# The next batch's token transposes go to the bank of the probabilities' transposes

## The chip, the cores and the metric

The kernel runs on one core of one Trainium2 chip. The metric is device time in microseconds of one execution; before and after are compared by medians of several runs.

## The reference

The reference is one transformer block over 16 batches of 256 tokens with 128 features, in float32. The attention half is what the change touches:

```
x = _layernorm(x)
q, k, v = x Wq, x Wk, x Wv            # 16 heads of 64
scores  = q k^T / sqrt(64), causal
attn    = softmax(scores)
heads   = attn v
y       = x + heads Wo, then a layernorm with gamma and beta
x       = x + _layernorm(y)
```

Then follows a router over 8 experts (softmax of `xt @ router_w`, the top 2), an expert layer `gelu(xt @ w1[e]) @ w2[e]` weighted with the gates, a last layer norm, and a residual sum.

## The kernel before

Attention runs over the 16 batches (`b`), each in four steps (`u` = 0 to 3), each step for two pairs of heads (`p`, `p + 1`; `k` counts steps over all batches). After the attention the expert part works on tiles of 256 rows. The order of the work is written out by hand for each engine, and the engines meet through semaphores.

Everything in one step is a pipeline over several engines. TensorE (the function `step` in the tensor block) does in this order: Q and K of the pair two ahead (`qk_proj`, L385 to L387, three products of split float32 values), the transposes of the normalised probabilities of an earlier pair (`p_transpose`, L442 to L447), the output projection (`w_o`, L434), the next `qk_proj`, the next `p_transpose` and `w_o`, a part of V (`v_proj`, L385 to L387 with 512 columns), the product of probabilities and V (`pv_two`, L423), and then scores and masks (L406, L409, L414) of the two next pairs. In step 1 of a batch it also does the transposes of the router's rows (L453), the router's logits (L460) and, between `pv_two` and the scores, the two 128x128 transposes of the next batch's tokens (`x_transpose`, L378).

ScalarE in the same step: the copy of Q and K out of PSUM (`qk_copy`, L1263), the exponentials of two pairs (L1268, L1274; each has an accumulator read behind it), the copies of the transposed probabilities (`pT0_copy`, L1279), the copy of V (`v_copy`, L1283), the copy of the attention's output (`o_copy`, L1288), and in step 1 the copy of the transposed tokens (`xt_copy`, L1258) and the router's exponential (L1297). VectorE: maxima of the scores (L777, L778), the division of the probabilities (L788, L792), the second half of the transposes' copies (L798), the norms (L755 for the tokens), and the split of the transposed tokens into a high and a low part (`x_split`, L770 and L772) in step 2.

PSUM has eight banks of 512 float32 per partition. Four hold scores (`SC`), and there is one each for `PT0` (transposes of the probabilities, in front of `pT0_copy`), `PT1O` (further transposes, and the attention's output), `M` (Q, K and V projections, and so far the token transposes) and `A` (output projection, router).

Semaphores that the text names: `v_done` counts copies of V; `xt_mm` and `xt_st` count token transposes and their copies; `xn_done` normalised tokens; `qk_sb` copies of Q and K; `exp_done` pairs whose exponentials are done; `pt0_sb` copies out of PT0; `nrm` normalised pairs; `xt_split` splits.

Of the kernel before, what the change touches and what calls it, by code (L numbers as in the profile page):

```python
# [14 lines left out]
P = 128  # L15
# [5 lines left out]
def sandwich_kernel(nc, x, wq, wk, wv, wo, gamma, beta, router_w, w1, w2, out):  # L21
    B, S, D = x.shape
    H, _, E = wq.shape
    NE, _, F = w1.shape
    T = S // P
    NP = H // 2
# [32 lines left out]
    with ExitStack() as ctx:  # L59
        def sb(name, shape, dt=F32):  # L60
            return ctx.enter_context(nc.sbuf_tensor(name, shape, dt))

        def bank(name):
            return ctx.enter_context(nc.psum_tensor(name, [P, 512], F32))
# [3 lines left out]
        def sem(name):  # L68
            if name not in sems:
                sems[name] = ctx.enter_context(nc.semaphore(name))  # L70
            return sems[name]
# [16 lines left out]
        ident = sb("ident", [P, P])  # L88
# [10 lines left out]
        xn = [sb(f"xn{n}", [P, T, D]) for n in range(2)]  # L99
        xt_st = sb("xt_st", [P, S])  # L100
# [87 lines left out]
        PT0, PT1O, M, A = (bank(n) for n in ("PT0", "PT1O", "M", "A"))  # L188
# [19 lines left out]
        v_mm, v_done = sem("v_mm"), sem("v_done")  # L208
# [14 lines left out]
        def before_out(attending):  # L223

            first = T * D if attending else T * D + 2 * T * NE
            return A[:, first:first + (T + 1) * NE]
# [14 lines left out]
        def there(b, back=0):  # L241

            return not isinstance(b, int) or 0 <= b - back < B
# [9 lines left out]
        def is_last(b):  # L253

            return isinstance(b, int) and b == B - 1
# [116 lines left out]
        def _(pe):  # L372
            mm = nc.tensor.matmul

            def x_transpose(b):
                pe.wait_ge(sem("xn_done"), b + 1)
                for t in range(T):
                    last = nc.tensor.transpose(M[:, t * P:(t + 1) * P], xn[b % 2][:, t, :], ident[:])  # L378
                last.then_inc(sem("xt_mm"), 1)

            pe.wait_ge(sem("ident_ok"), 1)
            x_transpose(0)

            def product3(dst, a_hi, a_lo, b_hi, b_lo, start=True):
                mm(dst, a_hi, b_hi, start=start, stop=False, skip_group_check=True)  # L385
# [3 lines left out]
            def qk_proj(c, dst=M):  # L389

                cs = slice(c * P, (c + 1) * P)
                for i in range(2):
                    last = product3(dst[:, i * S:(i + 1) * S], wqk_hi[:, i, cs], wqk_lo[:, i, cs],
                                    xt_hi[:], xt_lo[:], start=(i == 0))
                last.then_inc(qk_mm, 1)

            def v_proj(t, half_of_heads):
                cols = slice(half_of_heads * 512, half_of_heads * 512 + 512)
                ts = slice(t * P, (t + 1) * P)
                product3(M[:, :], xt_hi[:, ts], xt_lo[:, ts], wv_hi[:, cols], wv_lo[:, cols]).then_inc(v_mm, 1)  # L400
# [30 lines left out]
            def w_o(c):  # L431
                par = c % 2
                for t in range(T):
                    last = mm(A[:, t * D:(t + 1) * D], hT[:, par, t * P:(t + 1) * P], wo_sb[:, c, :],  # L434
                              start=(c == 0 and t == 0), stop=(c == NP - 1), skip_group_check=True)
                if c == NP - 1:
                    last.then_inc(sem("wo_mm"), 1)

            def p_transpose(p):
                slot, par = p % 4, p % 2  # L440
                for k in range(2):
                    last = nc.tensor.transpose(PT1O[:, par * S + k * P:par * S + (k + 1) * P], prob[:, slot, k, 2, :],  # L442
                                               ident[:])
                last.then_inc(t1_mm, 1)
                for k in range(2):
                    nc.tensor.transpose(PT0[:, k * S:k * S + P], prob[:, slot, k, 0, :], ident[:])  # L446
                    last = nc.tensor.transpose(PT0[:, k * S + P:(k + 1) * S], prob[:, slot, k, 1, :], ident[:])  # L447
                last.then_inc(t0_mm, 1)

            def rows_transpose(dst, r):  # L450
                pe.wait_ge(sem("xf_done"), r + 1)
                for t in range(T):
                    last = nc.tensor.transpose(dst[:, t * P:(t + 1) * P], xf[:, t, :], ident[:])  # L453
                last.then_inc(sem("xfT_mm"), 1)
# [25 lines left out]
            def step(b, u):  # L480


                k = STEPS * b + u
                p = 2 * k
                c = 2 * u
                more = u < STEPS - 1 or there(b, -1)

                if u == 1 and there(b, 2):
                    pe.wait_ge(pt0_sb, p - 2)
                    rows_transpose(PT0, b - 2)  # L490

                if more:
                    if k >= 1:
                        pe.wait_ge(v_done, 4 * b + 1 + u)
                    if u == 2 and there(b, -1):
                        pe.wait_ge(sem("xt_st"), b + 2)
                    if u == STEPS - 1:
                        pe.wait_ge(sem("xt_split"), b + 2)
                    if k == 1:
                        pe.wait_ge(sem("wqk_lo"), 4)  # L500
                    qk_proj((c + 2) % NP)

                if k >= 1:
                    pe.wait_ge(nrm, p - 1)
                    if k >= 2:
                        pe.wait_ge(o_sb, k - 1)
                        pe.wait_ge(pt0_sb, p - 2)
                    if u == 1 and there(b, 2):
                        pe.wait_ge(sem("xfT_sb"), b - 1)
                    p_transpose(p - 2)  # L510

                if k == 0:
                    pe.wait_ge(qk_sb, 3)
                    v_proj(0, 0)


                if k >= 2:
                    pe.wait_ge(o_sb, k - 1)
                    if u == 2 and there(b, 1):
                        pe.wait_ge(sem("att_done"), b)  # L520
                        if there(b, 2):
                            pe.wait_ge(sem("lg_done"), b - 1)
                    if u == 1 and there(b, 3):
                        pe.wait_ge(sem("before_sb"), b - 2)
                    w_o((c - 4) % NP)

                if more:
                    pe.wait_ge(qk_sb, p + 3)
                    if k == 0:
                        pe.wait_ge(v_done, 1)  # L530
                    qk_proj((c + 3) % NP)

                if k >= 1:
                    pe.wait_ge(nrm, p)
                    pe.wait_ge(pt0_sb, p - 1)
                    pe.wait_ge(pt1_sb, p - 1)
                    p_transpose(p - 1)

                if k >= 2:
                    w_o((c - 3) % NP)  # L540
                if u == 0 and there(b, 3):
                    rows_before(b - 3, before_out(True), False)
                if u == 1 and there(b, 2):
                    logits(b - 2, logits_out(True), False)
                if is_last(b) and u == STEPS - 1:
                    first_rows()

                turn = v_turn(b, u)
                if turn:
                    if more:  # L550
                        pe.wait_ge(qk_sb, p + 4)
                    v_proj(turn[0], turn[1])

                if k >= 1:
                    pe.wait_ge(pt0_sb, p)
                    pe.wait_ge(pt1_sb, p)
                    pe.wait_ge(v_done, 4 * b if u == 0 else 4 * b + 2 if u < 3 else 4 * b + 4)
                    pv_two((c - 2) % NP)


                if u == 1 and there(b, -1):
                    pe.wait_ge(v_done, 4 * b + 3)
                    x_transpose(b + 1)

                if more:
                    pe.wait_ge(qk_sb, p + 4)
                    pe.wait_ge(exp_done, p + 1)
                    scores(0)
                    pe.wait_ge(exp_done, p + 2)
                    scores(1)  # L570
                    masks(0)
                    masks(1)
# [155 lines left out]
            for g in range(NG):  # L728
# [3 lines left out]
                for r in range(K):  # L732
                    last = mm(sum_bank[g % 4][:], ident[:], zz[:, g % 4, r].rearrange("p t d -> p (t d)"),
                              start=(r == 0), stop=(r == K - 1))
# [517 lines left out]
        @block.scalar  # L1252
        def _(act):
            a = nc.scalar
            def xt_copy(b):
                act.wait_ge(sem("xt_mm"), b + 1)

                a.activation(xt_st[:].rearrange("d (p t) -> d t p", t=T), M[:, 0:S].rearrange("d (t p) -> d t p", t=T),  # L1258
                             ACT.Copy).then_inc(sem("xt_st"), 1)

            def qk_copy(p, src=M):
# [49 lines left out]
                        .then_inc(sem("wqk_h"), 1)  # L1311

            qk_high(0)
            xt_copy(0)
            act.wait_ge(sem("wv_ld"), 16)
            a.activation(wv_hi[:], wv_in[:], ACT.Copy).then_inc(sem("wv_h"), 1)
            qk_copy(0)
# [323 lines left out]
```

## Time and profile before

| | |
|---|---|
| median of 3 runs | 734.25 us (733.94 to 735.72) |
| profiled execution | 735.79 us |
| its span | 734.0 us |
| TensorE busy | 687.1 us, 94% of the span |
| VectorE busy | 553.2 us, 75% |
| ScalarE busy | 521.7 us, 71% |
| mean granted TensorE clock | 0.984 |

The span is the time from the profile's first to its last instruction; the device time holds a little more. Busy time is time in which the engine works on an instruction; the ends of matmuls are modelled, so starts are the safer numbers.

### The profile page before, as it was taken

How to read it: one execution, taken by the hardware profiler on the slowest of the kernel's cores; microseconds unless marked ns; L12 is line 12 of the kernel's file. 1: busy time of each engine (PE TensorE's matmuls, PEld its weight loads, DVE VectorE, ACT ScalarE, POOL GpSimd, SP SyncE). 2: the span in 40 equal slices, each digit the busy share in tenths (PEclk: the TensorE clock that was granted, in tenths of full speed). 3: DMA queues.
4: the chain of work that ended last, by engine and by line, in shares of the span. 5: the costliest groups of instructions: out<-in, count | busy, mean ns of one | idle time of the engine just before them, and what ended most of it. 6: DMA issues, size and time to landing. Idle time of an engine off the chain costs nothing.

```text
span 734.0 us, 17696 instructions
## 1 busy us (share of the span) xinstructions
PE 687.1 (94%) x5954; PEld 593.1 (81%) x5955; DVE 553.2 (75%) x1914; ACT 521.7 (71%) x1687; POOL 273.2 (37%) x388
## 2 busy tenths in 40 slices
PE   4899999999999999999999999999989999999954
PEld 3688878888888888887888888888868999999921
DVE  5667889888797989888887989898886775444216
ACT  4787777888787877888877878788765664555515
POOL 3022634332323232332323231322322877655535
PEclk9999999999999999999999999999999999999978
DMA  7530000000000000000100000000020234322155
GB/s 182 173 87 8 9 8 12 21 21 18 24 8 23 9 24 8 25 15 16 31 8 23 9 23 8 24 15 10 21 56 24 73 104 132 91 74 84 41 184 174
DMA packets 43701, 34.88 MB, mean 48 GB/s; under 512 B 10624, under 2 KB 40320, under 8 KB 43616
## 3 DMA queue, kind: packets, MB, share of 16 engines
q1 hardware_dynamic: 37984, 23.81, 12.1%
q0 software_dynamic: 4544, 9.45, 3.6%
q8 instruction: 47, 0.77, 0.4%
q10 hardware_dynamic: 1088, 0.54, 0.3%
q14 instruction: 38, 0.31, 0.1%
HBM read 20.22 MB, written 13.56 MB: 46 GB/s over the span
## 4 chain that ended last, share of the span: by engine, by line
PE 65%; ACT 14%; DVE 12%; DMA 3%; issue 3%; POOL 2%; DVEq 1%; SPq 0%; POOLq 0%; ACTq 0%
PE M L684 8%; PE SC L406 8%; PE PT1O L423 8%; PE A L434 5%; PE M L385 4%; ACT prob L1274 4%; PE M L387 4%; PE M L386 4%; PE SC L414 4%; PE SC L409 3%; ACT prob L1268 3%; ACT qk L1263 3%; PE PT1O L442 2%; PE SC L385 2%; PE SC L386 2%
## 5 line engine op out<-in xcount | busy, mean ns | idle before, releaser
L1263 ACT ACTIVATE qk<-M 128x512 f32<-128x512 f32 x127 | 75.9, 598 | 90.0 <-PE M L387 90.0
L1274 ACT ACTIVATE prob<-SC,nmax 128x256 f32<-128x256 f32 x256 | 125.7, 491 | 0.0
L423 PE MATMUL PT1O<-pT,v_sb 128*64 128x256 f32 (+1 forms) x1024 | 98.6, 335 | 0.7 <-ACT pT L1279 0.7
L423 PEld LDWEIGHTS PT1O<-pT,v_sb 128*64 128x64 f32 x1024 | 64.1, 138 | 42.8 <-ACT pT L1279 17.2
L1268 ACT ACTIVATE prob<-SC,nmax 128x128 f32<-128x128 f32 x256 | 95.4, 382 | 3.4 <-DVE nmax L778 3.3
L1544 POOL DMA_INDIRECT expert_rows<-v_sb,got x78 | 77.1, 988 | 46.5 <-ACT v_sb L1418 27.7
L788 DVE TENSOR_TENSOR prob<-prob,rden 128x512 f32<-128x512 f32 x128 | 88.8, 694 | 2.4 <-DVE rden L782 0.2
L1533 POOL DMA_INDIRECT sent_rows<-rec,slot x64 | 66.6, 1040 | 57.7 <-DVE slot L1038 39.3
L778 DVE TENSOR_REDUCE nmax<-SC 128x2 f32<-128x512 f32 x128 | 86.9, 679 | 0.0
L385 PE MATMUL M<-xt_hi,wqk_hi 128*128 128x256 f32 x254 | 82.5, 325 | 3.0 <-DVE xt_lo L772 2.2
L406 PE MATMUL SC<-qk 64*128 64x256 f32 x512 | 84.4, 406 | 0.6 <-ACT prob L1274 0.6
L777 DVE TENSOR_REDUCE nmax<-SC 128x2 f32<-128x256 f32 x128 | 53.1, 415 | 38.6 <-PE SC L414 38.3
L1279 ACT ACTIVATE pT<-PT 128x512 f32<-128x512 f32 x128 | 76.6, 598 | 3.3 <-PE PT L447 3.3
L434 PE MATMUL A<-wo_sb,hT 128*128 128x128 f32 x512 | 77.8, 275 | 0.0
L684 PE MATMUL M<-w_sb,hidT 128*128 x624 | 76.2, 275 | 0.9 <-ACT v_sb L1418 0.9
L684 PEld LDWEIGHTS M<-w_sb,hidT 128*128 128x128 f32 x624 | 72.7, 192 | 1.1 <-issue 1.1
L387 PE MATMUL M<-xt_hi,wqk_lo 128*128 128x256 f32 x254 | 72.1, 284 | 0.0
L386 PE MATMUL M<-xt_lo,wqk_hi 128*128 128x256 f32 x254 | 71.6, 282 | 0.0
L434 PEld LDWEIGHTS A<-wo_sb,hT 128*128 128x128 f32 x512 | 67.1, 192 | 0.0
L447 PE MATMUL PT<-ident,prob 128*128 128x128 f32 x256 | 62.8, 273 | 0.0
L446 PE MATMUL PT<-ident,prob 128*128 128x128 f32 x256 | 62.8, 273 | 0.0
L1418 ACT ACTIVATE v_sb<-M,got 128x128 f32<-128x128 f32 x78 | 24.4, 364 | 52.3 <-PE M L684 52.3
(186 smaller groups left out, 1777.8 us busy)
## 6 DMA issues: line engine op xcount, KB each, us to landing
got<-sent_rows SPq DMA_DIRECT2D x39, 132.0 KB, 2.3
w_in<-expert_rows SPq DMA_DIRECT2D x16, 256.0 KB, 3.6
x_in<-L_attn_x SPq DMA_DIRECT2D x16, 128.0 KB, 2.2
w_in<-L_ffn_w SPq DMA_DIRECT2D x1, 2048.0 KB, 11.6
x_res<-L_attn_x SPq DMA_DIRECT2D x16, 128.0 KB, 2.1
w_sb<-L_ffn_w SPq DMA_DIRECT2D x8, 256.0 KB, 4.8
out<-y_out SPq DMA_DIRECT2D x8, 256.0 KB, 2.1
sent_rows<-pad_rec SPq DMA_DIRECT2D x11, 132.0 KB, 4.5
```

Of the source, the lines that this page charges most:

```text
L385: mm(dst, a_hi, b_hi, start=start, stop=False, skip_group_check=True)
L386: mm(dst, a_hi, b_lo, start=False, stop=False, skip_group_check=True)
L387: return mm(dst, a_lo, b_hi, start=False, stop=True, skip_group_check=True)
L406: mm(SC[par][:, k, LATE_Q], qk[r, par, 0, P:S], qk[r, par, 1, :], start=True, stop=False, skip_group_check=True)
L423: last = mm(PT1O[k * E:(k + 1) * E, cols], v_sb[:, t, h * E:(h + 1) * E], src[:, par, k, :], start=(t == 0), stop=(t == 1), skip_group_che ...
L434: last = mm(A[:, t * D:(t + 1) * D], hT[:, par, t * P:(t + 1) * P], wo_sb[:, c, :], start=(c == 0 and t == 0), stop=(c == NP - 1), skip_gr ...
L684: last = mm(out_bank[:, t * D:(t + 1) * D], hidT[:, s, c, t * P:(t + 1) * P], w2_e[:, c * D:(c + 1) * D], start=(t == 0 and c == 0), stop= ...
L778: v.tensor_reduce(nmax[:, par, 0, :], SC[par][:, :, LATE_Q], AX_X, ALU.max, negate=True).then_inc(mx, 1)
L788: v.tensor_tensor(prob[:, slot, :, 1:3, :], prob[:, slot, :, 1:3, :], rden[:, par, 0, :].unsqueeze(2).unsqueeze(3).broadcast_to([P, 2, 2, ...
L1263: a.activation(qk[:, p % 2], src[:].rearrange("p (i s) -> p i s", i=2), ACT.Copy).then_inc(qk_sb, 1)
L1268: return a.activation(prob[:, slot, k, 0, :], SC[par][:, k, EARLY_Q], ACT.Exp, bias=nmax[:, par, 1, k:k + 1], accum_out=den[:, par, 1, k:k ...
L1274: return a.activation(prob[:, slot, k, 1:3, :].rearrange("p n t -> p (n t)"), SC[par][:, k, LATE_Q], ACT.Exp, bias=nmax[:, par, 0, k:k + 1 ...
```

## The change

The token transposes of batches 1 to 15 are written into PT0 instead of M, and ScalarE's copy reads PT0. The wait for the copy of V in front of them goes. The wait for the copy of the transposed tokens moves, in step 2, from the projections (which write M) to the transposes of the probabilities (which write PT0). Batch 0's tokens, ahead of the loop, stay in M.

```diff
-            def x_transpose(b):
+            def x_transpose(b, dst=PT0):
                 pe.wait_ge(sem("xn_done"), b + 1)
                 for t in range(T):
-                    last = nc.tensor.transpose(M[:, t * P:(t + 1) * P], xn[b % 2][:, t, :], ident[:])
+                    last = nc.tensor.transpose(dst[:, t * P:(t + 1) * P], xn[b % 2][:, t, :], ident[:])
                 last.then_inc(sem("xt_mm"), 1)
 
             pe.wait_ge(sem("ident_ok"), 1)
-            x_transpose(0)
+            x_transpose(0, M)
...
                 if more:
                     if k >= 1:
                         pe.wait_ge(v_done, 4 * b + 1 + u)
-                    if u == 2 and there(b, -1):
-                        pe.wait_ge(sem("xt_st"), b + 2)
...
                     if u == 1 and there(b, 2):
                         pe.wait_ge(sem("xfT_sb"), b - 1)
+                    if u == 2 and there(b, -1):
+                        pe.wait_ge(sem("xt_st"), b + 2)
                     p_transpose(p - 2)
...
                 if u == 1 and there(b, -1):
-                    pe.wait_ge(v_done, 4 * b + 3)
                     x_transpose(b + 1)
...
-            def xt_copy(b):
+            def xt_copy(b, src=PT0):
                 act.wait_ge(sem("xt_mm"), b + 1)
 
-                a.activation(xt_st[:].rearrange("d (p t) -> d t p", t=T), M[:, 0:S].rearrange("d (t p) -> d t p", t=T),
+                a.activation(xt_st[:].rearrange("d (p t) -> d t p", t=T), src[:, 0:S].rearrange("d (t p) -> d t p", t=T),
                              ACT.Copy).then_inc(sem("xt_st"), 1)
...
-            xt_copy(0)
+            xt_copy(0, M)
```

## Rows read from the trace of the kernel before

**Rows 1.** The page, busy time of each engine.

```profile
PE 687.1 (94%) x5954; PEld 593.1 (81%) x5955; DVE 553.2 (75%) x1914; ACT 521.7 (71%) x1687; POOL 273.2 (37%) x388
```

**Rows 2.** One batch: length, busy PE, PEld, DVE, ACT, POOL, PEclk, DMA, GB/s.

```profile
297.50:330.70 33.20, 32.83 (x300) 27.99 (x299) 28.70 (x103) 26.68 (x95) 9.89 (x16) 1.00 0.06 18
```

**Rows 3.** TensorE's waits, whole span: us in total, times, longest.

```profile
PE M L378 <- ACT v_sb L1283: 6.6, 15, 0.9
PE PT1O L442 <- DVE prob L792: 4.3, 5, 2.2
PE M L385 <- DVE xt_lo L772: 2.2, 2, 1.3
```

**Rows 4.** TensorE in order of time: start, duration, instruction; batches 0, 1 and 9.

```profile
28.37 1.52 PE L423 MATMUL PT1O<-pT,v_sb 128*64 128x256 f32 x16
30.81 0.44 PE L378 MATMUL M<-ident,xn 128*128 128x128 f32 x2 [0.92 <-ACT v_sb L1283]
...
61.06 1.52 PE L423 MATMUL PT1O<-pT,v_sb 128*64 128x256 f32 x16
63.41 0.44 PE L378 MATMUL M<-ident,xn 128*128 128x128 f32 x2 [0.83 <-ACT v_sb L1283]
...
330.68 1.52 PE L423 MATMUL PT1O<-pT,v_sb 128*64 128x256 f32 x16
332.57 0.44 PE L378 MATMUL M<-ident,xn 128*128 128x128 f32 x2 [0.37 <-ACT v_sb L1283]
332.94 0.70 PE L406 MATMUL SC<-qk 64*128 64x256 f32 x4
...
333.70 0.60 PE L406 MATMUL SC<-qk 64*128 64x256 f32 x4
...
334.82 0.36 PE L385 MATMUL M<-xt_hi,wqk_hi 128*128 128x256 f32 x1
...
335.61 0.38 PE L442 MATMUL PT1O<-ident,prob 128*128 128x128 f32 x2
```

**Rows 5.** TensorE in order of time, a step without token transposes.

```profile
306.12 1.52 PE L423 MATMUL PT1O<-pT,v_sb 128*64 128x256 f32 x16
307.57 0.70 PE L406 MATMUL SC<-qk 64*128 64x256 f32 x4
```

**Rows 6.** ScalarE in order of time, batch 0 (first row) and batch 9.

```profile
29.99 0.28 ACT L1274 ACTIVATION_READ_ACCUMULATOR prob<-SC,nmax 128x1 f32 x1
...
331.79 0.25 ACT L1274 ACTIVATION_READ_ACCUMULATOR prob<-SC,nmax 128x1 f32 x1
331.88 0.64 ACT L1283 ACTIVATE v_sb<-M 128x512 f32<-128x512 f32 x1
...
332.36 0.65 ACT L1288 ACTIVATE hT<-PT1O 128x512 f32<-128x512 f32 x1
...
333.11 0.40 ACT L1258 ACTIVATE xt_st<-M 128x256 f32<-128x256 f32 x1
...
335.81 0.60 ACT L1263 ACTIVATE qk<-M 128x512 f32<-128x512 f32 x1 [2.20 <-PE M L387]
```

**Rows 7.** VectorE in order of time, batch 9.

```profile
330.75 0.60 DVE L755 TENSOR_SCALAR xn<-x_in,mv_x,rstd_x 128x128 f32<-128x128 f32 x2
...
334.88 0.42 DVE L777 TENSOR_REDUCE nmax<-SC 128x2 f32<-128x256 f32 x1 [1.61 <-PE SC L414]
```

**Rows 8.** TensorE's weight loads in order of time, the last batch's last step.

```profile
558.81 1.28 PEld L423 LDWEIGHTS PT1O<-pT,v_sb 128*64 128x64 f32 x16 [0.93 <-ACT pT L1279]
560.26 0.20 PEld L657 LDWEIGHTS PT<-ident,got 128*128 128x128 f32 x2 [0.17 <-issue]
```

**Rows 9.** TensorE's weight loads in order of time, two places.

```profile
307.57 0.30 PEld L406 LDWEIGHTS SC<-qk 64*128 64x128 f32 x4 [0.17 <-issue]
...
325.43 0.25 PEld L453 LDWEIGHTS PT<-ident,xf 128*128 128x128 f32 x2
...
325.65 0.19 PEld L385 LDWEIGHTS M<-xt_hi,wqk_hi 128*128 128x128 f32 x1
```

## The prediction

> **What bounds the kernel now.** I read the page first: TensorE is busy for 94% of the span, the next engine for 75% [rows 1]. [...] Then the waits of TensorE: of all its idle time in the attention part, the only entry that comes back in every batch is "PE M L378 <- ACT v_sb L1283", 15 times, 6.6 us in all, 0.9 us at the longest [rows 3]. Everything else there is once or a few times. So inside a batch TensorE is the bound except at one place, the transposes of the next batch's tokens (L378), which stand still until ScalarE has copied V out of the projections' bank (L1283). The change works on this place.
>
> **What the place looks like.** In batch 9 the matmuls with the probabilities (L423) start at 330.68, the transposes at 332.57, the next scores (L406) at 332.94 [rows 4]. In a step without the token transposes the scores follow the same sixteen matmuls after 307.57 - 306.12 = 1.45 us [rows 5]. Here the transposes follow after 1.89 us. ScalarE ends its last exponential at 331.79 + 0.25 = 332.04, copies V from 331.88 to 332.52, and TensorE goes on 0.05 us later [rows 6].
>
> **Part 1, the wait taken away in front of the transposes (v_done, L562).** With the probabilities' bank as target, the transposes need only three things. First, their tokens: VectorE has them at 330.75 + 0.60 = 331.35 [rows 7], 0.78 us before they would be used. Second, the bank: its last reader is the copy of the transposed probabilities, and the code waits for that one (pt0_sb, L555) in front of L423 already, so nothing is left to wait for behind L423. Third, TensorE itself, at 330.68 + 1.45 = 332.13. That 1.45 also holds where the next instruction is a 128*128 transpose and not a 64*128 score: at 558.81 the same sixteen weight loads are followed by transposes of L657 at 560.26, again 1.45 us, with 0.17 us of "issue" between the loads [rows 8]. So the transposes start at 332.13 and not at 332.57: 0.44 us.
>
> The starts of the other batches give the rest. The pattern of batch 9, a distance of 1.89 or 1.90 us from L423 to L378, is that of all thirteen batches from 2 to 14 [rows 4]: 13 x 0.445 = 5.8 us. Batch 0: 30.81 - 28.37 = 2.44, so 0.99 us. Batch 1: 63.41 - 61.06 = 2.35, so 0.90 us. Sum 5.8 + 0.99 + 0.90 = 7.7 us. The profile's own idle figure, 6.6 us for the fifteen [rows 3], is the low end: it counts from the modelled end of the last matmul, and I take starts, since starts are what moves.
>
> **Part 2, from the transposes to the scores.** This is 332.94 - 332.57 = 0.37 us now [rows 4]. The scores wait for qk_sb and exp_done. The first scores need the first pair's exponentials, which ScalarE does before the second pair's; the second scores need the second pair's, done at 332.04; the new starts are 332.13 + 0.37 = 332.50 and, 0.76 us later (333.70 - 332.94), 333.26 [rows 4, 6]. So the second has 1.2 us to spare. In batch 0 the last exponential ends at 29.99 + 0.28 = 30.27 [rows 6], the second scores would start at 28.37 + 1.45 + 0.37 + 0.76 = 30.95: 0.7 us to spare. The 0.37 could shrink: the two row transposes of L453 are followed by their neighbour's weight load 0.22 us after theirs [rows 9]. That would be 15 x 0.15 = 2.2 us more, the top end. I take zero, because before L406 the loads show 0.17 us of "issue" after L423 too, where nothing stood still [rows 9]: the gap belongs to the change of tile form and not to the stall.
>
> [...]
>
> **Part 3, the xt_st wait, moved in step 2 of a batch from the projections to the probability transposes.** In front of the projections (L385 at 334.82) the wait cost nothing: the copy L1258 ran from 333.11 to 333.51. Removing it there gives nothing. In its new place it stands before L442 at 335.61, which comes at 335.17 after the change [rows 4, 6]. Behind it on TensorE are the rest of the transposes, the sums of L434 and the next projection, so a late copy would stop all of them. But ScalarE now starts L1258 directly behind the copy L1288 (which ends at 333.01), since its transposes are done by 332.5: it ends by 333.4, 1.8 us early. Cover gone, each 0.1 us of lateness would cost 15 x 0.1 = 1.5 us. Zero. The wait for v_done in front of the projections stays; V is copied at 332.52 and they now start at 334.38.
>
> **Part 4, who is late next.** Everything after the scores moves forward by 0.44 us per batch, if the others can follow. ScalarE then waits 2.20 us for the first projection of the step [rows 6], VectorE 1.61 us for the scores [rows 7]. Both wait for TensorE, and after the change for 1.76 and 1.17 us. So they do not become the bound. The loads of tokens, the sends and the statistics are started by these engines and move with them. No instruction other than waits is added or removed; no DMA moves; batch 15 has no such transposes, and the first batch's keep the projections' bank. The expert part starts from the same engines' last instructions, so it moves as a whole.
>
> **Sum.** 7.7 us. The profiled execution took 735.79 us, its span 734.0, so 1.79 us lie around the span; it is 1.54 us above the median of the runs shown, 734.25. Taken off the profiled execution that is 728.1, off the median **726.5 us**, 1.05% faster.
>
> **The rivals.**
> *As summed* (0.80): 6.6 to 9.9 us off, 724.3 to 727.7.
> *Partly kept* (0.06): in the early batches TensorE also waits for VectorE (over the whole span L442 on prob five times, 4.3 us, L385 on xt_lo twice, 2.2 us [rows 3]). If these waits are set by something that does not move, the two large stalls of batches 0 and 1 and a few more (3 to 4 us) come back there: about 730. Against it: VectorE's chain in these batches starts from scores too.
> *Weight loads run ahead* (0.03): no gap at either side of the transposes, 15 x (0.17 + 0.15) = 4.8 us more, 12.5 in all, 721.8 us. Against: [rows 8, 9]. [...]
> *Absorbed, no change* (0.08): some other wait takes all of it. The nearest candidates are the exponentials in front of the second scores (spare 1.2 us, 0.7 in batch 0) and the tokens (spare 0.78 us); either would have to be late by the whole spare and by 0.4 us more. Or the expert part's start hangs on something that does not move. 734 us.
> *Slower* (0.03): the moved wait decides. From 1.8 us of lateness of L1258 on it costs, and to outdo the gain and show by 0.3% it would need 7.7 + 2.2 = 9.9 us, 0.66 us per batch, so a copy 2.5 us late; at 2.7 us late the price is 15 x 0.9 = 13.5, and the time 740 us. Nothing stands on ScalarE between L1288 and L1258 that could do this [rows 6].
>
> **How the numbers follow.** 0.3%, 2.2 us, is about what a measurement of this kernel can tell from no change. The likeliest case's own range is 724.3 to 727.7; the range that should hold 8 in 10 takes in its bounds, some scatter of the medians (the three runs lie 1.8 us apart), and the nearer half of the partly kept case: 724.0 to 729.5. Faster: 0.80 + 0.06 + 0.03 = 0.89, same 0.08, slower 0.03.
>
> **What the profile after should show.** L378 no longer waits for L1283; L423 to L378 is 1.45 us in all fifteen batches; L378 to L406 still 0.37; batch length 32.76 where it was 33.20; ScalarE's idle time before the projections' copy in step 2 near 1.76 and VectorE's before L777 near 1.17; L1258 ends well before L442. The prediction is wrong if L378 waits for xn (L755), if L406 waits for prob, if L442 waits for xt_st in step 2, or if the steady batches stay 33.20 us long.

## The result, and the profile after

The changed kernel takes 727.53 us (median of 8 runs, 725.79 to 731.28), the kernel before 734.01 us in the same comparison (8 runs, 732.98 to 735.72). The ratio is 0.9909, with a 95% interval of 0.9887 to 0.9931: 6.5 us less by the medians, where 7.7 were forecast. The profiled execution of the changed kernel took 728.19 us, its span went from 734.0 to 726.4 us, 7.6 us less. In the changed file ScalarE's and VectorE's lines have numbers one lower than before (the copy of V is L1282, that of the tokens L1257, the norm of the tokens L754), and TensorE's up to L447 have the same.

TensorE's waits over the whole span (us in total, times, longest). This answers to [rows 3]:

```profile
PE M L378 <- DVE xn L754: 7.9, 1, 7.9
PE PT1O L442 <- DVE prob L791: 4.3, 5, 2.2
PE M L385 <- DVE xt_lo L771: 2.2, 2, 1.3
```

The wait of L378 for the copy of V, 15 times and 6.6 us, is gone. The other two of [rows 3] are there to the tenth of a microsecond; the first row here is the start of the kernel, batch 0's tokens, and stood in the trace of before as well, with 7.7 us.

TensorE in order of time, batches 0, 9 and 14. This answers to [rows 4]:

```profile
27.92 1.52 PE L423 MATMUL PT1O<-pT,v_sb 128*64 128x256 f32 x16
29.37 0.44 PE L378 MATMUL PT<-ident,xn 128*128 128x128 f32 x2
...
325.14 1.52 PE L423 MATMUL PT1O<-pT,v_sb 128*64 128x256 f32 x16
326.59 0.44 PE L378 MATMUL PT<-ident,xn 128*128 128x128 f32 x2
326.96 0.70 PE L406 MATMUL SC<-qk 64*128 64x256 f32 x4
...
329.63 0.38 PE L442 MATMUL PT1O<-ident,prob 128*128 128x128 f32 x2
...
489.30 1.52 PE L423 MATMUL PT1O<-pT,v_sb 128*64 128x256 f32 x16
490.75 0.44 PE L378 MATMUL PT<-ident,xn 128*128 128x128 f32 x2
```

Subtract the starts. From L423 to L378 it is 29.37 - 27.92 = 1.45 us in batch 0, where it was 2.44, and 1.45 in batches 9 and 14, where it was 1.89 and 1.90. It is 1.45 in the other twelve as well. From L378 to L406 it is 0.37 us as before.

ScalarE in order of time, batch 9. This answers to [rows 6]:

```profile
326.34 0.64 ACT L1282 ACTIVATE v_sb<-M 128x512 f32<-128x512 f32 x1
326.82 0.65 ACT L1287 ACTIVATE hT<-PT1O 128x512 f32<-128x512 f32 x1
327.29 0.47 ACT L1257 ACTIVATE xt_st<-PT 128x256 f32<-128x256 f32 x1
...
329.83 0.60 ACT L1262 ACTIVATE qk<-M 128x512 f32<-128x512 f32 x1 [1.98 <-PE M L387]
```

The transposes (326.59) now begin while the copy of V is only 0.25 us old. The copy of the tokens ends at 327.76, 1.87 us ahead of L442.

VectorE in order of time, batch 9. This answers to [rows 7]:

```profile
325.20 0.60 DVE L754 TENSOR_SCALAR xn<-x_in,mv_x,rstd_x 128x128 f32<-128x128 f32 x2
...
328.90 0.42 DVE L776 TENSOR_REDUCE nmax<-SC 128x2 f32<-128x256 f32 x1 [1.17 <-PE SC L414]
```

Its wait for the scores was 1.61 us and is 1.17.

TensorE's weight loads in order of time, batch 9. This answers to [rows 8, 9]:

```profile
326.58 0.20 PEld L378 LDWEIGHTS PT<-ident,xn 128*128 128x128 f32 x2 [0.17 <-issue]
326.95 0.30 PEld L406 LDWEIGHTS SC<-qk 64*128 64x128 f32 x4 [0.17 <-issue]
```

The gap of 0.17 us stands ahead of the transposes although nothing is left for them to wait for.

The length of one batch, which answers to [rows 2] (length, busy PE, PEld, DVE, ACT, POOL, PEclk, DMA share, GB/s):

```profile
292.37:325.14 32.77, 32.77 (x299) 27.99 (x298) 28.72 (x103) 26.62 (x96) 9.93 (x16) 1.00 0.06 18
```

The window of [rows 2] was set 0.04 us late at one end and 0.02 at the other; by the starts of L423 that batch took 330.68 - 297.46 = 33.22 us. So a batch went from 33.22 to 32.77 us, TensorE is now busy in all of it, and the granted clock is 1.00 in both.

**Where the time went.** Batch 14's transposes start at 490.75 instead of 498.98, 8.23 us earlier. Of these 0.45 us are the start of the kernel (L423 of batch 0 at 27.92 instead of 28.37, which differs from profile to profile, 27.81 to 29.08 over the fourteen traces), so the fifteen batches gave 7.8 us. Behind these transposes 0.7 us are handed back (the span is 7.6 us shorter, not 8.23). The load of the last results shows 0.4 of it: TensorE waits 1.09 us for it where it waited 0.69.

```profile
714.68 1.98 PE L732 MATMUL SC<-w_in,ident 128*128 128x512 f32 x4 [1.09 <-DMA w_in<-expert_rows]
```

**Where the scatter sits.** The attention part repeats from trace to trace, the part behind it does not. From batch 0's L423 to batch 14's L378 it is 470.61 us before and 462.83 after, 7.8 us less, and in two more traces (before_again and again_2 below) 470.70 and 462.84. From batch 14's L423 to the last L423, of batch 15, it is 61.7 us before and 61.3 after, but 58.8 and 58.6 in those two, in which the granted clock did not fall there (1.00 from 530 to 560 us in both). The stretch from 530 to 560 us, first in the changed kernel's trace, then in again_2's:

```profile
530.00:560.00 30.00, 26.58 (x216) 22.87 (x215) 21.96 (x85) 17.56 (x51) 6.97 (x11) 0.89 0.19 46
530.00:560.00 30.00, 26.51 (x238) 23.37 (x237) 24.27 (x92) 19.60 (x56) 8.13 (x12) 1.00 0.20 50
```

In about as much busy time TensorE did 216 instructions at a mean granted clock of 0.89, and 238 at 1.00. The traces of before and after both have this fall (0.89 from 530 to 560 us in both), so their spans compare like with like; a run that has it is some 3 us longer than one that hasn't (61.7 - 58.8 = 2.9, 61.3 - 58.6 = 2.7).

### The profile page after: what moved, and what is told of

Its sections match the earlier page's. It is cut to its first block, busy times and chain, and to the rows that moved or that the text cites. A ratio compares the mean times of both kernels' runs of the same rounds, so it can differ in the third digit from the quotient of the medians.

```text
span 726.4 us, 17681 instructions
## 1 busy us (share of the span) xinstructions
PE 685.2 (94%) x5954; PEld 592.6 (82%) x5955; DVE 554.1 (76%) x1914; ACT 520.7 (72%) x1687; POOL 273.6 (38%) x388
## 4 chain that ended last, share of the span: by engine, by line
PE 78%; DVE 12%; DMA 3%; ACT 2%; issue 2%; DVEq 1%; POOL 1%; SPq 0%; POOLq 0%; ACTq 0%
PE PT1O L423 11%; PE M L683 9%; PE SC L406 8%; PE A L434 6%; PE M L385 5%; PE M L387 5%; PE M L386 5%; PE SC L414 4%; PE PT1O L442 3%; PE SC L409 3%; PE PT L447 3%; PE PT L446 3%; PE SC L385 3%; PE SC L386 2%; PE SC L387 2%
## 5 line engine op out<-in xcount | busy, mean ns | idle before, releaser
L423 PE MATMUL PT1O<-pT,v_sb 128*64 128x256 f32 (+1 forms) x1024 | 98.6, 335 | 0.7 <-ACT pT L1278 0.7
L423 PEld LDWEIGHTS PT1O<-pT,v_sb 128*64 128x64 f32 x1024 | 64.0, 138 | 43.0 <-ACT pT L1278 17.4
L385 PE MATMUL M<-xt_hi,wqk_hi 128*128 128x256 f32 x254 | 82.5, 325 | 3.0 <-DVE xt_lo L771 2.2
L406 PE MATMUL SC<-qk 64*128 64x256 f32 x512 | 83.9, 404 | 0.6 <-ACT prob L1273 0.6
L447 PE MATMUL PT<-ident,prob 128*128 128x128 f32 x256 | 62.8, 273 | 0.0
```

The costliest lines, as they stand in the source:

```text
L406: mm(SC[par][:, k, LATE_Q], qk[r, par, 0, P:S], qk[r, par, 1, :], start=True, stop=False, skip_group_check=True)
L423: last = mm(PT1O[k * E:(k + 1) * E, cols], v_sb[:, t, h * E:(h + 1) * E], src[:, par, k, :], start=(t == 0), stop=(t == 1), skip_group_che ...
```

## The experiments

Three groups of four kernels ran, each with the kernel before beside them: group 1 (again, behind_masks, wait_not_moved, bank_only) on one chip, where the kernel before took 757.55 us; group 2 (before_again, tokens_first, behind_masks_M, wait_for_o) and group 3 (again_2, behind_masks_2, late_copy_2, late_copy_5) on two others, with 734.31 and 734.08 us. Ratios are to the kernel before of the same group.

**1. The changed kernel again** (again, group 1; again_2, group 3).

> The changed kernel once more, beside the others of this group, as their reference. Theory (the gain is the stall in front of L378, moved rigidly to the end): 6.5 to 7.7 us off the kernel before, about 727. If the first measurement was low or high by the scatter of its runs (725.8 to 731.3), this one says so.

> The changed kernel once more, for the others of this group. The first group's trace (another chip) had the tokens late in eleven batches, the very first trace of the changed kernel in none. Where att starts 0.6 us ahead of L423, this run should show 1.45 us from L423 to L378 in all fifteen batches and 0.989 of before; where att starts 0.5 us behind L423, 1.83 us and 0.991.

Measured: 750.94 us in group 1, ratio 0.9914 (0.9891 to 0.9936), 6.6 us less; 725.34 us in group 3, ratio 0.9876 (0.9857 to 0.9895), 8.7 us less. The trace of group 3 has 1.45 or 1.46 us from L423 to L378 in all fifteen batches, as expected where `att` is early; the 0.989 lies inside the interval. The trace of group 1 is another picture. TensorE's waits there:

```profile
PE PT L378 <- DVE xn L754: 3.9, 11, 0.8
```

and TensorE in order of time in batch 9:

```profile
327.10 1.52 PE L423 MATMUL PT1O<-pT,v_sb 128*64 128x256 f32 x16
328.93 0.44 PE L378 MATMUL PT<-ident,xn 128*128 128x128 f32 x2 [0.32 <-DVE xn L754]
```

From batch 4 on the transposes come 1.82 to 1.89 us behind L423 (2.28 in batch 14) and wait for their tokens. VectorE in order of time shows why the tokens are late:

```profile
327.58 0.42 DVE L1053 TENSOR_TENSOR att<-xn,A 128x256 f32<-128x256 f32 x1 [1.87 <-PE A L460]
...
328.28 0.60 DVE L754 TENSOR_SCALAR xn<-x_in,mv_x,rstd_x 128x128 f32<-128x128 f32 x2
```

The sum `att` (L1053) begins 0.48 us behind L423; in the first trace of the changed kernel it begins 0.63 us ahead of it (324.51 against 325.14), though TensorE's logits (L460), for which it waits, end 0.73 to 0.74 us ahead of L423 in both. The tokens stand behind `att` on VectorE. So on that chip a second wait lay right behind the one removed, and the transposes start 0.38 us later than they could (1.83 against 1.45) in most of these eleven batches. The old wait cost more there too, 2.05 us in bank_only below, so a steady batch still gained 0.2 us. By the traces of bank_only and again the distance from batch 0's L423 to batch 14's L378 shrank by 472.94 - 467.93 = 5.0 us and not by 7.8. The 6.6 us of the medians is more than that; the rest lies behind the attention part and is not explained.

**2. The wait alone, the bank alone** (group 1).

```diff
# bank_only, on top of the change
                 if u == 1 and there(b, -1):
+                    pe.wait_ge(v_done, 4 * b + 3)
                     x_transpose(b + 1)
# wait_not_moved, on top of the change
                         pe.wait_ge(v_done, 4 * b + 1 + u)
+                    if u == 2 and there(b, -1):
+                        pe.wait_ge(sem("xt_st"), b + 2)
...
-                    if u == 2 and there(b, -1):
-                        pe.wait_ge(sem("xt_st"), b + 2)
                     p_transpose(p - 2)
```

> The transposes go to PT0, and the wait for xt_st is moved, but the wait for the copy of V in front of the transposes stays. Theory A (the gain is that wait alone): the time of the kernel before, 734, and 1.89 us again from L423 to L378 in steady batches, 0.99 and 0.90 us more than 1.45 in batches 0 and 1. Theory B (the bank itself matters, by reads and writes that get out of each other's way): between 727 and 734.

> The changed kernel with the wait for xt_st back in its old place, in front of the projections of step 2 and not of L442. Theory A (that wait costs nothing in either place, the copy is done 1.1 us ahead of the projections): the same time as the changed kernel, about 727, span 726.4 within 0.5. Theory B (part of the gain comes from the projections no longer waiting for the copy): back by some us, up to 734, with an idle time in front of L385 that ends at the copy L1258.

Measured: bank_only 756.99 us, ratio 0.9993 (0.9976 to 1.001); wait_not_moved 751.88 us, ratio 0.9936 (0.9913 to 0.9958), beside 750.94 for the changed kernel, with intervals that overlap. In bank_only batches 0 to 3 have the old distances to 0.01 us (2.44, 2.35, 1.89, 1.89); from batch 4 on they are 2.03 to 2.10 and not 1.89, since `att` is late in that trace too. In wait_not_moved the first three distances from L378 to L378 are those of the changed kernel to 0.01 us (31.71, 33.37, 35.03 against 31.71, 33.37, 35.02), and the steady batches of the shortest kind are 33.11 to 33.20 us against 33.14 to 33.18. The absolute times that the expectations name, 727 and 734, don't hold on that chip; the ratios do. So the bank by itself is worth nothing that shows (the interval leaves room for 1.8 us), the moved wait costs nothing at either place (467.79 us to batch 14's L378, 467.93 in the changed kernel), and the gain is the wait in front of the transposes.

**3. A longer stall at the same place** (wait_for_o, group 2).

```diff
                 if u == 1 and there(b, -1):
+                    pe.wait_ge(o_sb, k)
                     x_transpose(b + 1)
```

> The changed kernel with one more wait in front of the transposes: for the copy of the attention's output, which ends 0.49 us behind that of V in the trace of before. Theory (each stall at this place goes to the end in full, in all fifteen batches): L378 at 1.89 + 0.49 = 2.38 us behind L423 in steady batches, 15 x 0.49 = 7.3 us more than the kernel before, 1.010 of it. Rival (some of it is taken up by later slack): less than 1.005.

Measured: 741.57 us, ratio 1.0099 (1.0079 to 1.0118), 7.3 us more than before. TensorE in order of time:

```profile
334.83 1.52 PE L423 MATMUL PT1O<-pT,v_sb 128*64 128x256 f32 x16
337.21 0.44 PE L378 MATMUL PT<-ident,xn 128*128 128x128 f32 x2 [0.86 <-ACT hT L1288]
```

337.21 - 334.83 = 2.38 us, as forecast. With before (1.89) and after (1.45) this gives three points on a line: from batch 0's L423 to batch 14's L378 it is 462.8, 470.6 and 477.9 us. What the transposes lose or gain here, times fifteen, is in the time, and no later slack takes any of it up.

**4. Another place for the transposes** (behind_masks, groups 1 and 3; behind_masks_M, group 2).

```diff
# behind_masks, on top of the change; behind_masks_M: the same move in the kernel before, the wait for v_done moves along
-                if u == 1 and there(b, -1):
-                    x_transpose(b + 1)
...
                     masks(0)
                     masks(1)
+                if u == 1 and there(b, -1):
+                    x_transpose(b + 1)
```

> The token transposes stand behind the masks of step 1, in front of the next projection, both of the same 128*128 form, and still go to PT0. Theory A (the 0.15 us between the transposes and the scores belong to the change of tile form): the transposes cost 0.22 us instead of 0.37, so 15 x 0.15 = 2.2 us less than the changed kernel, about 725. The copy has then 1.0 us until L442, needs about 0.88, so it just fits. Theory B (the 0.15 us belong to the waits that stand there, and move along with the transposes): the same time as the changed kernel, about 727. Theory C: the copy doesn't fit and L442 waits for xt_st, each 0.1 us costing 1.5 us: 728 or more.

> The transposes behind the masks, in PT0, beside the changed kernel. In the first group it was 5.7 us of span below the changed kernel (741.0 against 746.8), 0.54 us in a steady batch, of which 0.38 us was the wait for late tokens that this place is free of. Theory: where the tokens are on time, what is left is the 0.15 us of the tile form, 15 x 0.15 = 2.2 us below the changed kernel of this group, 0.986; where they are late, 5 to 6 us, 0.984. Rival (the place is worth more than that for another reason): over 4 us although the tokens are on time.

> The kernel before (target M) with only the place of the token transposes moved behind the masks; V has long been copied there, but the next projection writes M too and has to wait for the copy of the tokens. Theory (the bank is what lets the place be free): no wait in front of L378, but one of 0.7 to 0.8 us in front of L385 in each of 15 batches; a steady batch takes 32.62 + 0.8 = 33.4 us, so the time of the kernel before within 3 us, and some 12 us more than the same place with PT0. Rival (the place alone gives the gain, the copy being short): 0.985 of before, as with PT0.

Measured: 744.27 us in group 1, ratio 0.9838 (0.9815 to 0.9862), 6.7 us below the changed kernel; 723.93 us in group 3, ratio 0.986 (0.9841 to 0.9879), 1.4 us below it by the medians and 2.3 by the spans (721.8 against 724.1). A steady batch takes 32.61 to 32.63 us on both chips, where the changed kernel takes 32.77 on the one and 33.16 on the other. TensorE and its loads in order of time in behind_masks of group 1:

```profile
326.90 0.61 PE L414 MATMUL SC<-mask,ident_bf 128*128 128x256 bf16 x4
327.24 0.25 PEld L378 LDWEIGHTS PT<-ident,xn 128*128 128x128 f32 x2
...
327.46 0.19 PEld L385 LDWEIGHTS M<-xt_hi,wqk_hi 128*128 128x128 f32 x1
...
328.38 0.41 PE L442 MATMUL PT1O<-ident,prob 128*128 128x128 f32 x2
```

The form is the pair that a line of the profile gives ahead of the shape, 128\*128 for L414, L378, L385 and L442 here, 128\*64 for L423, 64\*128 for L406. Between instructions of the same 128\*128 form there is no 0.17 us of "issue" on either side, and the next load follows 0.22 us after. Theory A holds: 0.15 us per batch go away with the change of form, and by starts batch 14's L423 comes 2.5 us sooner in group 3 (458.93 us behind batch 0's, against 461.38). That move changes the neighbours as well as the form, so the other loads of the trace have to say which of the two it is. In the first 520 us of the changed kernel's trace each of the 200 loads behind another form starts after a gap of at least 0.12 us (0.17 in all 45 L406 behind L423, 0.12 in all 62 L414 behind L409); of the 4317 behind a load of their own form only 17 have a gap that long, and 13 of these wait for ScalarE or VectorE. So the gap goes with the change of form; what makes it, no run shows. In group 1, where tokens were late, the place gave 0.54 us in a steady batch, since the tokens have 1.6 us more there.

With M as the target in the same place, the time is 734.7 us, ratio 1.0006 (0.9994 to 1.0018):

```profile
334.10 0.38 PE L378 MATMUL M<-ident,xn 128*128 128x128 f32 x2
335.11 0.36 PE L385 MATMUL M<-xt_hi,wqk_hi 128*128 128x256 f32 x1 [0.64 <-ACT xt_st L1259]
```

The wait for V moved along and costs nothing there, as expected. But the projection that writes the same bank now waits 0.64 us for the tokens' copy in each batch (9.6 us over fifteen), a little less than the 0.7 to 0.8 expected. So the other bank is worth nothing in the old order with the old wait, and everything where the order would otherwise run into a reader.

**5. A late copy of the tokens** (group 3). N = 2 or 5 idle copies ahead of it; they add work and leave nothing out.

```diff
                     act.wait_ge(sem("xt_split"), b + 1)
+                    # scratch is a new [128, 512] buffer in SBUF
+                    for j in range(N):
+                        if b or j:
+                            act.wait_ge(sem("dummy"), N * b + j)
+                        a.activation(scratch[:], wv_in[:, 0:512], ACT.Copy).then_inc(sem("dummy"), 1)
                     xt_copy(b + 1)
```

> The changed kernel with two idle copies (128 x 512, into a scratch buffer, each waiting for the one before) on ScalarE ahead of the copy of the tokens: about 2 x 0.64 = 1.3 us later. Theory (the moved wait has 1.8 us of spare time, and ScalarE 1.8 to 2.0 us before the next projection): the same time as the changed kernel within 1 us, and no wait in front of L442. Rival (the moved wait is tight): some us more, and L442 waits for xt_st.

> The same with five idle copies, 3.2 us. Theory: this is 1.4 us beyond the spare time, so L442 waits for xt_st by about that, and 15 x 1.4 = 21 us are added to the changed kernel: about 1.02 of the kernel before. Rival (the copy's lateness is taken up elsewhere): under 5 us more than with two.

Measured: 725.72 us with two (changed kernel 725.34), ratio 0.9885 (0.9866 to 0.9904); 748.08 us with five, ratio 1.0183 (1.016 to 1.0205), 22.7 us more than the changed kernel. With two, L442 waits for nothing and has 0.68 us to spare. TensorE in order of time with five, and its waits:

```profile
345.95 0.41 PE L443 MATMUL PT1O<-ident,prob 128*128 128x128 f32 x2 [1.27 <-ACT xt_st L1258]
```

```profile
PE PT1O L443 <- ACT xt_st L1258: 20.0, 15, 1.8
```

The five copies move the end of the tokens' copy from 2.62 to 5.78 us behind batch 9's first row of probabilities times V, 3.16 us, and TensorE stands still for 1.27 of them: the spare time of the moved wait is 1.9 us, and past it each microsecond costs fifteen. Batch 0 paid more, 3.58 us (35.30 from start to start instead of 31.72), for a stall of 1.81:

```profile
34.89 0.58 PE L443 MATMUL PT1O<-ident,prob 128*128 128x128 f32 x2 [1.81 <-ACT xt_st L1258]
```

From there to 38.26 us the granted clock was 0.51, where it was 1.00 from 28.40 to 34.89, and two transposes that take 0.38 or 0.41 us elsewhere took 0.58. So about 1.8 us of the 22.7 (3.58 - 1.81) are the clock behind the stall and not the stall.

**6. Are late tokens a matter of the kernel?** (before_again and tokens_first, group 2).

```diff
-        xn = [sb(f"xn{n}", [P, T, D]) for n in range(2)]
+        xn = [sb(f"xn{n}", [P, T, D]) for n in range(3)]   # and xn[b % 3] for xn[b % 2] throughout
...
                 if u == 1:
+                    if there(b, -1):
+                        x_normalise(b + 1)
                     if there(b, 1):
                         attended(b - 1)
...
-                    if there(b, -1):
-                        x_normalise(b + 1)
...
-                if b >= 2:
-                    dve.wait_ge(sem("att_done"), b - 1)
+                if b >= 3:
+                    dve.wait_ge(sem("att_done"), b - 2)
```

> The kernel before, for its trace beside the others of this group. In the first group the tokens' norm (L755) ended 1.8 us behind the start of L423 from batch 4 on, against 0.67 us in the first trace of before. If that is a state of the chip and not of the changed kernel, this trace shows it too: att (L1054) at 0.5 us behind L423 instead of 0.6 us ahead of it, and L378 at 2.0 to 2.1 us behind L423 instead of 1.89.

> The changed kernel with three token buffers, so that VectorE normalises the next tokens ahead of att instead of behind it. In the first group's trace of the changed kernel, L378 waited for these tokens in eleven batches (1.83 us behind L423 instead of 1.45). Theory A (what is late is att, which waits for TensorE and then starts 1.1 us late, and the tokens only stand behind it): the tokens are ready in time, 1.45 us in all batches, and where att is late the time is 11 x 0.38 = 4 us less than the changed kernel's, so 0.986 of before; where att isn't late, the same as the changed kernel. Theory B (VectorE stops there whatever comes next): the tokens are as late as before and the ratio stays at 0.991.

Measured: before_again 733.51 us in its one run, with `att` 0.6 us ahead of L423 and L378 at 1.89 or 1.90 us in all batches from 2 on: this group's chip does not show the late `att`. tokens_first took 724.87 us, ratio 0.9863 (0.9843 to 0.9883). Its tokens are ready 1.0 us ahead of L423 instead of 0.67 us behind it, and its steady batches, 32.79 us, are as long as the changed kernel's. Where `att` is on time, that is what both theories gave. No changed kernel ran beside it; against the first comparison's 0.9909 its ratio looks better, but to batch 14's L378 it gains only 0.2 us (462.67 against 462.83), so the rest is the scatter behind the attention part. The case that would part them did not come up again, so whether the tokens would be on time on the first group's chip stays open.

## Why the prediction was right

**Part 1, 7.7 us, the wait in front of the transposes.** Right in each term: 1.45 us in all fifteen batches of the profiled run, 7.8 us measured at batch 14 against 7.7. That bank_only is at 0.9993 shows that it is this wait, and wait_for_o at 1.0099 that every stall here goes to the end in full. The rival *partly kept* is out: TensorE's waits for VectorE in the early batches are unchanged (4.3 and 2.2 us in both traces), and batches 0 and 1 got shorter by 0.97 and 0.93 us (32.69 to 31.72, 34.29 to 33.36). Taking starts and not the idle figure of 6.6 us was the better choice.

**Part 2, 0.37 us, nothing gained.** Right. The reason given, that the gap goes with the tile form, is borne out by behind_masks (0.22 us from L378's load to the next, where it was 0.37) and by the other changes of form in the trace (at least 0.12 us at all 200). The rival *weight loads run ahead*, no gap at either side of the transposes, is out: 0.17 us stand ahead of L378's load and 0.17 ahead of L406's in each of the fifteen batches.

**Part 3, the moved wait, 0 us with 1.8 us to spare.** Right: 1.87 us in the trace; two idle copies cost nothing (0.4 us by the medians), five cost 22.7 us.

**Part 4, who is late next.** VectorE's 1.17 us came out to the digit. ScalarE's is 1.98 us and not 1.76: its copy of the tokens no longer waits and starts 0.47 us behind the start of the copy in front of it instead of 0.75, so that ScalarE is done 0.21 us sooner. The prediction used this in Part 3 and forgot it here; it also had the copy start at the end of the one in front, where in the trace it starts 0.18 us before that end (327.29, and 326.82 + 0.65 = 327.47). The spare time of 0.78 us for the tokens was there in four profiles of the changed order (the first, again_2 and both with idle copies), but on the chip of group 1 (again, wait_not_moved) it was used up by an `att` 1.1 us late. This is the condition that the prediction named ("if L378 waits for xn"). It is why a steady batch there gained 0.2 us against bank_only (33.16 against 33.37) and not 0.44. The other chips' gain holds because their `att` is early, which the prediction read from one trace and did not know to be a matter of the chip.

**The sum.** 6.5, 6.6 and 8.7 us in three comparisons, around the 7.7. The runs of one kernel in one comparison spread over up to 5.5 us, more than the differences between the three. The first comparison's changed kernel spreads most, with a run of 731.28 us at a mean granted clock of 0.938, where its others have 0.984 to 0.990. So 6.5 against 7.7 says nothing against the terms, which the starts confirm to 0.1 us. The 6.6 of group 1 is no confirmation: the starts there give 5.0, and it came near the forecast by scatter or by something in the expert part.

## What to carry to other kernels

When a stall on the bound engine is released by a copy that only frees a buffer, give the instruction another free bank; the gain here was the distance between starts, stall by stall, against a neighbour that does not wait, times the count. Then list every other thing that the instruction waits for, with its spare time: the smallest, here 0.78 us, is the next bound, and another chip may already be there. A place between instructions of its own tile form was the cheaper one for this small matmul, and a later place helps against late inputs as well: behind the masks the transposes took 0.15 us less per batch and did not feel the late tokens. That kernel (0.9838 and 0.986 of before) has the lowest median on both chips where it ran; it is clear of the changed kernel on the first, while on the second the intervals overlap. To compare two variants this close, compare starts in the part that changed, since the rest of the span scatters by 3 us.

## What was not expected of the hardware

On one of the chips VectorE's `att` started 1.1 us later than on the others from batch 4 on, with TensorE's and GpSimd's instructions around it at the same distances (in batches 4 to 13 the logits' end 0.73 to 0.74 us ahead of L423, and GpSimd's fourth indirect DMA 0.46 us ahead of it). It starts within 0.06 us of the end of that DMA's issue in batches 4 to 13, but in batch 14 it does not (in again it starts 0.93 us behind L423, and that issue ends 0.06 us ahead of L423), and in batch 3 it runs while such an issue is under way. On the other chips `att` starts on time beside the same issues (0.62 or 0.63 us ahead of L423 from batch 4 on in the first trace of the changed kernel, before_again and again_2). So a block by GpSimd is a guess that the traces do not bear out throughout; the cause stays open. The same chip was about 3% slower for each of the three kernels that ran on another one too (757.55 against 734.31 us for the kernel before, 750.94 against 725.34 for the changed one, 744.27 against 723.93 with the transposes behind the masks), and of the first only about 3 us lie ahead of batch 14's transposes (501.70 in bank_only against 498.98 before); some 20 us lie behind the last L423 (195.96 us from there to the end in bank_only, 175.17 before), in the expert part, and were not looked into.
